# First product of an FFN kernel: hi and lo matmuls issued in pairs of contraction steps

## What is computed

```
w = weight[adapter_ids]
return jnp.einsum('bsi,boi->bso', x, w)
...
logits = x_flat @ gate_w.T + expert_bias
top1 = jnp.argmax(logits, axis=-1)
base_out = jnp.einsum('bth,oh->bto', x, W_up)
z = jnp.einsum('nh,erh->ner', x_flat, lora_A)
d = jnp.einsum('ner,ehr->neh', z, lora_B) * SCALE
delta = jnp.einsum('neh,ne->nh', d, one_hot)
```

## Time and profile before

| | us |
|---|---|
| median of 3 runs | 386.61 (386.48 to 386.88) |
| the profiled execution | 386.45 |
| its span, first to last instruction | 384.4 |
| PE busy / PEld busy in it | 375.4 / 317.2 |
| DVE busy / ACT busy in it | 263.5 / 163.0 |
| chain: share of L745, of L747 | 26.5%, 13.4% |

### The profile page before, as it was taken

How to read it: one execution, slowest core, us unless ns; L and a number is a source line. 1 busy time by engine, 2 the same in 40 slices (tenths; PEclk the granted TensorE clock), 3 DMA queues, 4 the chain that set the end, 5 groups by cost and what they waited for, 6 DMA issues and landing times.

```text
span 384.4 us, 5419 instructions
## 1 busy us (share of the span) xinstructions
PE 375.4 (98%) x1946; PEld 317.2 (83%) x1946; DVE 263.5 (69%) x501; ACT 163.0 (42%) x329; POOL 4.7 (1%) x15
## 2 busy tenths in 40 slices
PE   6999999999999999999999999999999999999996
PEld 5888888888888788887888878888888878888885
DVE  4878766787658997579636795477864788446743
ACT  5658524554146623565114642255412554044300
POOL 1000200000000000000000000000000000000000
PEclk9999999999999999999999999999999999999999
DMA  7999946860089600875037640476304861160002
GB/s 240 413 378 353 410 192 220 319 226 2 0 309 333 233 2 14 287 271 195 2 122 247 234 163 2 165 282 202 119 0 175 318 218 59 49 226 0 2 0 109
DMA packets 19081, 68.12 MB, mean 177 GB/s; under 512 B 2288, under 2 KB 2416, under 8 KB 19056
## 3 DMA queue, kind: packets, MB, share of 16 engines
q1 hardware_dynamic: 18768, 66.74, 48.4%
q10 hardware_dynamic: 288, 1.05, 0.8%
HBM read 59.39 MB, written 8.39 MB: 176 GB/s over the span
## 4 chain that ended last, share of the span: by engine, by line
PE 83%; DMA 5%; DVE 3%; issue 3%; ACT 2%; SPq 1%; POOLq 1%; POOL 0%; DVEq 0%
PE ps_y L745 26%; PE ps_y L747 13%; PE ps_u L752 6%; PE ps_u L754 5%; PE ps_u L756 5%; DMA gl_raw<-gl_dram 4%; PE ps_g L765 4%; PE ps_v L752 4%; PE ps_v L756 4%; PE ps_v L754 4%; PE ps_p L752 2%; PE ps_p L754 2%; PE ps_p L756 2%; DVE w_lo L488 2%; ACT w_hi L346 1%
## 5 line engine op out<-in xcount | busy, mean ns | idle before, releaser
L745 PE MATMUL ps_y<-x_hilo,w_hi 128*128 128x512 f32 x512 | 181.0, 398 | 1.4 <-DVE w_lo L481 1.1
L747 PE MATMUL ps_y<-x_hilo,w_lo 128*128 128x256 f32 x512 | 143.7, 281 | 0.0
L745 PEld LDWEIGHTS ps_y<-x_hilo,w_hi 128*128 128x128 f32 x512 | 96.1, 188 | 25.6 <-DVE w_lo L481 1.5
L747 PEld LDWEIGHTS ps_y<-x_hilo,w_lo 128*128 128x128 f32 x512 | 96.7, 189 | 0.3
L488 DVE TENSOR_TENSOR w_lo<-w_raw,w_hi 128x512 fp32r<-128x512 f32 x126 | 81.2, 687 | 16.7 <-ACT w_hi L346 15.7
L361 ACT COPY small<-ps_y 128x256 f32<-128x256 f32 x64 | 23.8, 372 | 116.4 <-PE ps_y L747 116.4
L346 ACT CAST w_hi<-w_raw 128x512 fp32r<-128x512 f32 x126 | 71.8, 623 | 0.7 <-DMA w_raw<-w_dram 0.7
L533 DVE TENSOR_TENSOR y_raw<-ps_y,small 128x256 f32<-128x256 f32 x64 | 27.1, 423 | 52.4 <-ACT small L361 52.3
L752 PE MATMUL ps_u<-up_hi,y_parts 128*128 128x512 f32 x112 | 44.6, 398 | 0.0
L754 PE MATMUL ps_u<-up_lo,y_parts 128*128 128x512 f32 x112 | 43.8, 391 | 0.0
L756 PE MATMUL ps_u<-up_hi,y_parts 128*128 128x512 f32 x112 | 43.7, 390 | 0.0
(11 more groups left out here) (81 smaller groups left out, 355.5 us busy)
## 6 DMA issues: line engine op xcount, KB each, us to landing
w_raw<-w_dram SPq DMA_DIRECT2D x64, 512.0 KB, 4.4
rows<-x_dram SPq DMA_DIRECT2D x16, 512.0 KB, 5.8
out_dram<-rows SPq DMA_DIRECT2D x15, 512.0 KB, 2.6
x_raw<-xT_dram SPq DMA_DIRECT2D x14, 512.0 KB, 5.0
up_raw<-w_up_dram SPq DMA_DIRECT2D x8, 512.0 KB, 11.6
up_stage<-w_up_dram SPq DMA_DIRECT2D x8, 512.0 KB, 13.9
x_raw<-xT_dram ACTq DMA_DIRECT2D x2, 512.0 KB, 4.3
lb_raw<-lora_b_dram SPq DMA_DIRECT2D x4, 128.0 KB, 13.9
```

Of the source, the lines that this page charges most:

```text
L745: pe.matmul(ps_y[c % 2][:, :], w_hi[:, n % RING, cols], x_hilo[:, :, k, :], start=(k == 0), stop=False)
L747: last = pe.matmul(ps_y[c % 2][:, S:2 * S], w_lo[:, n % RAWS, cols], x_hilo[:, 0, k, :], start=False, stop=(k == KC - 1))
```

## The change

In `first_product` the body of the loop over `k` issues matmuls at even `k` only, and then for two steps: 512 columns with `w_hi` for `k` and for `k + 1`, then 256 columns with `w_lo` for `k` and for `k + 1`. The matmuls, their operands, their number (512 of each kind) and the bank are the same; the sums are taken in another order. The waits keep their places ahead of the even steps.

```
-                        cols = slice(k * P, (k + 1) * P)
-                        pe.matmul(ps_y[c % 2][:, :], w_hi[:, n % RING, cols], x_hilo[:, :, k, :],
-                                  start=(k == 0), stop=False)
-                        last = pe.matmul(ps_y[c % 2][:, S:2 * S], w_lo[:, n % RAWS, cols], x_hilo[:, 0, k, :],
-                                         start=False, stop=(k == KC - 1))
+                        if k % 2 == 0:
+                            for i in (k, k + 1):
+                                pe.matmul(ps_y[c % 2][:, :], w_hi[:, n % RING, i * P:(i + 1) * P], x_hilo[:, :, i, :],
+                                          start=(i == 0), stop=False)
+                            for i in (k, k + 1):
+                                last = pe.matmul(ps_y[c % 2][:, S:2 * S], w_lo[:, n % RAWS, i * P:(i + 1) * P],
+                                                 x_hilo[:, 0, i, :], start=False, stop=(i == KC - 1))
```

## The result

| | us | ratio to the kernel before |
|---|---|---|
| before, median of 5 runs on the same chip | 386.76 (386.48 to 387.20) | |
| twos, median of 5 runs | 384.49 (383.95 to 385.00) | 0.9941 (0.9931 to 0.9952) |
| twos again, on another chip, 5 runs | 384.21 (383.83 to 384.92) | 0.9940 (0.9927 to 0.9954) |

The change makes the kernel faster by 0.6%, 2.3 us. The profiled execution took 384.51 us with a span of 382.5, against 386.45 and 384.4.

The account below looks back on a forecast made before the run. PE's matmul rate was taken as the bound. A group of 467 + 2 x 118 = 703 ns, times 256, gave 180.0 us against 180.5; minus 0.5 from the 386.61 median gave 386.1 us, range 384.0 to 388.3.

Parts of the forecast that it names:

- the likeliest case: First product: a group of two pairs takes 703 ns (698 to 708), 0.5 us gained, 386.1 us; chance 0.45.
- one of the prediction's own signs of being wrong: First product: PE settling at a rhythm outside 698 to 708 ns per group would show the prediction wrong.
- the first rival: First product: excess paid once per change from short to long; group 690 to 698 ns, 383.8 us; chance 0.22.
- PE's rate sets the end, an edit of its order counts in full, and the waits keep their places.: Whole kernel: PE busy 375.4 of 384.4 us, its matmuls' waits only 5.6 us, all ahead of even steps.
- Something in the rate is neither columns nor data and can settle at one value or another.: First product: the same pairs take 347 ns in batch 0 and 353 ns in batch 1.
- Two long matmuls in a group: 467 ns.: First product: two long matmuls behind a short one take 467 ns, against 470 in the alternation.
- Two short ones: 2 x 118 = 236.: First product: two short matmuls in a row cost 118 ns each, as in the alternation, nothing won or lost.
- the ends: First product: bounds kept for a short matmul's 118 ns, 112 and 125, the latter for a late weight load.
- Batch 0 loses 10 ns a group, 0.3 us.: Batch 0's first product: 10 ns lost in each of 32 groups, if its fast rhythm of 693 ns is lost.
- Gain swallowed in batch 2, 0.04 us.: Late in batch 2, where PE waits for DVE: three blocks of four groups lose their 3.5 ns, 0.04 us.
- Own columns only (386.6).: First product: a matmul costs by its own columns whatever stands beside it; time unchanged, 386.6 us; chance 0.13.
- Slower, with two H at 0.48 us.: First product: paired short matmuls disturb the following long ones more; group 713 ns, 2.0 us more, 388.6; chance 0.20.

Follow-up runs that it names:

- the repeat: The changed kernel (twos) measured again, on another chip: 384.21 us, ratio 0.9940 to the kernel before.
- the last two runs: Kernel before with other beginnings of the alternation in chosen batches, batch 5 HLLHHLLH (H long, L short) in both; batch 0 in twos in the second: 385.49, 385.64 us.
- the narrower weights: First product with 64-column weights in batches 1, 3, 5, 6, 7, and batch 4's long matmuls cut to 256 columns (all but step 0): 378.52 us in one run.
- the eights: Kernel before with all blocks of the first product as eight long matmuls, then eight short: 384.83 us, ratio 0.9953.
- fours: Kernel before with all blocks of the first product as four long matmuls, then four short: 385.33 us, ratio 0.9966.

## Why the prediction was right, and where its terms were off

The forecast was 386.1 us in 384.0 to 388.3; 384.5 was measured. The range held it, and "faster" was the likeliest of the three outcomes (0.42), but the likeliest case gave 0.5 us of gain and 2.3 were found. The time lies just outside that case's own bounds (384.8 to 387.4), and the group, 697 ns, just under its 698 to 708: one of the prediction's own signs of being wrong was met, by some 1 ns. That the range reached down to 384.0 was owed to half of the first rival, whose mechanism didn't occur, so the hit was in part luck. Step by step:

- *PE's rate sets the end, an edit of its order counts in full, and the waits keep their places.* Right. The ledger closes on the first products and the landing of the first transfer, and the list of waits is the old one but for 0.1 us in batch 2 and the entry ahead of the first block.
- *Something in the rate is neither columns nor data and can settle at one value or another.* Right, and it turned out to be the main thing; the prediction saw it in batch 0 and then treated it as a property of batch 0.
- *Two long matmuls in a group: 467 ns.* Right: 0.465. The second H does pay (in the trace's stamps of 1 ns both H of a group take 233 on average), and the rival by which it is clean (227) fails in its mechanism, though its size, 697 a group against 690 to 698, is the one that came out.
- *Two short ones: 2 x 118 = 236.* Here the working was off. Measured are 0.23 us (57.79 to 58.02 and 58.48 to 58.71), on average 230.5 ns in the trace's stamps. The gates' sixteen L with 72-column weights, which I took as the nearest row, were no bound from below; 112 stood among the ends and 118 was chosen. It is 5.5 ns a group, 5.5 x 224 = 1.2 us of the 1.8 that were missing; the H pair, 1 ns under its term, adds 0.2.
- *Batch 0 loses 10 ns a group, 0.3 us.* Wrong as a term. In the profiled execution its rhythm went from 346.7 to 348.3 only, 0.1 us. But the kernel before has the fast rhythm there in some executions alone (eight profiles of this study have an alternation in batch 0, the kernel before and seven variants; its middle blocks run at 346.7 in three of them, one of which has an exchange there, and at 353.1 to 353.4 in five), so in executions of the second kind the twos gain in batch 0 instead of losing. The other 0.25 us that batch 0 took longer in the profile is a wait for weights whose transfer landed later (ACT began on them at 10.20 after 0.68 us of waiting for the transfer, against 9.89 after 0.20 before). No list of waits shows it, because the matmul ahead is still in the pipeline: an L pair is followed by its H after 0.39 us instead of 0.23, and that H pair takes 0.56.

```profile
11.29 0.39 PE L749 MATMUL ps_y<-x_hilo,w_lo 128*128 128x256 f32 x2
11.68 0.73 PE L746 MATMUL ps_y<-x_hilo,w_hi 128*128 128x512 f32 x2
...
12.24 0.28 PE L749 MATMUL ps_y<-x_hilo,w_lo 128*128 128x256 f32 x1
```

  In the repeat the same batch took 22.48 us. The two together may account for the profiled spans differing by 1.9 and the medians by 2.3; that wasn't measured apart.
- *Gain swallowed in batch 2, 0.04 us.* Right in place, and larger with the larger gain: 0.15 us were won there instead of 0.31, and PE's wait for DVE grew from 0.3 to 0.4 us.
- *Own columns only (386.6).* Excluded: the same 16 matmuls of a block cost 348 to 353 ns a pair by their order alone. The Trainium skill, "TensorE: Matmul & The Clock Gate", "Back-to-back issue gap", gives its formula for an isolated matmul and, for streams, says that loads and matmuls set the spacing together; neither has a term for the order of long and short ones, and by these runs one is needed.
- *Slower, with two H at 0.48 us.* Did not occur.

What sets the rhythm is not settled. Shown are: it depends on the pattern, on the way in and, as far as batch 5 of the last two runs can show it, on differences of 0.01 us or less; a narrow load under the short matmul removes nearly all of what the alternation has over 227 + 113 (341.7); and an excess stays where the short matmul is much longer than the load's 0.11 us (16 ns at 384 columns). It also matters what is called an excess. The 113 ns of a short matmul was seen with a long one beside it; short ones behind each other with 128-column weights take 119 to 120 (batch 4 of the narrower weights; the eights). An H of 227 and an L of 119 to 120 make 346 to 347, which is the fast alternation: against uniform runs only the slow rhythm has an excess, some 6 ns. And in the slow rhythm the pairs are not alike. Every third takes 0.36 us and the two between 0.35, here in batch 3 of the kernel before:

```profile
155.29 0.40 PE L745 MATMUL ps_y<-x_hilo,w_hi 128*128 128x512 f32 x1
...
155.64 0.40 PE L745 MATMUL ps_y<-x_hilo,w_hi 128*128 128x512 f32 x1
...
155.99 0.40 PE L745 MATMUL ps_y<-x_hilo,w_hi 128*128 128x512 f32 x1
...
156.35 0.40 PE L745 MATMUL ps_y<-x_hilo,w_hi 128*128 128x512 f32 x1
```

What makes every third pair late stays open. A model that gives 353.1, 346.7, 348.3, 349.5, 350.5 and 348.8 from these was not found.

## What to carry to other kernels

When PE is the bound and a loop alternates long and short matmuls, measure start to start over a whole stage, divide by the count, and compare that with the same matmuls in uniform runs; the order of independent matmuls is then worth trying in twos, since it cost nothing else and gave 1.4% of the loop's rate here (353.1 to 348.3). Try several group sizes, since the gain doesn't grow with the group: fours were slower than twos. And compare the same stage of several executions before calling a rate typical: one profile may show a rhythm that the next execution doesn't have.

## What was not expected of the hardware

- The same alternation of 512- and 256-column matmuls runs at 346.7 or at 353.1 to 353.4 ns per pair, for as long as it isn't disturbed. One exchange of two neighbouring matmuls at a batch's start led to the fast one behind the `plain` batches, and one in the middle of such a batch ended it.
- Each repeating order has its own rate, for twos the same to 0.1 ns in every batch of four profiles in which it was undisturbed: twos 348.3, fours 350.8, eights 349.2 a pair in the middle of a batch.
- Narrower weights (64 columns instead of 128) made the alternation faster, 341.7 (H's), 347.5 (L's) and 342.5 (both), and the twos slower, 349.9 and 351.4 against 348.3.
- Short matmuls of 384 columns left a larger excess over their columns (16 ns) than those of 256 (13 ns over 227 + 113) although they are longer against the load beside them; those of 320 and 448 columns left 8 and 9 ns.
